# A new order of the steps of an attention group, for all engines

## The reference

```
xn = layernorm(x)
q = xn w_q (16 heads of 128), k, v = xn w_kv (4 groups of 128)
ctx = softmax(causal(q k^T / sqrt(128))) v        # 4 heads share one k, v
routed: 32 experts of 256, 6 per token by sigmoid scores in 4 of 8 groups
out = x + ctx w_dense + sum_e gate_e relu(xn W1_e^T)^2 W2_e^T
        + relu(xn Ws1^T)^2 Ws2^T
```

## The kernel before

| step | TensorE | ScalarE | VectorE |
|---|---|---|---|
| K, P, Q | project keys, values, queries of 512 tokens, 12 matmuls (L663 to L665, ps_s<-xT) | hi part | lo part (not P) |
| X | turn the values, 8 transposes (L955) | v_hi | v_lo |
| S | scores of one head and row, 3 or 6 matmuls (L974 to L976) | | |
| M | | | mask, negated row maximum, scores to probs (L1700) |
| E | | exponential and row sum (L1292) | |
| N | | | reciprocal of the sum (L1706), scaling (L1709) |
| T | turn one block of probabilities of four heads, 4 transposes (L987) | pT_hi (L1300) | pT_lo (L1319) |
| V | context of the block, 3 matmuls (bank<-pT) | | |
| F | | cT_hi | cT_lo |
| D | output projection, 12 matmuls (bank<-wa,cT) | | add to acc (L1740) |
| W | | hi of a fifth of the group's weights (araw) | lo |
| C | | | add one gathered expert output (L1729) |
| G | | | gate weights, first group only (L1507 to L1520) |

## Time and profile before

### The profile page before, as it was taken

One profiled execution on the slowest core, in us unless ns is written; L12 is line 12 of the kernel. 1 busy time (PEld: TensorE's weight loads), 2 busy tenths in 40 slices (PEclk: granted clock), 3 DMA queues, 4 the chain that ended last, 5 costly groups with the idle time before them and its releaser, 6 DMA issues.

```text
span 1565.0 us, 31168 instructions
## 1 busy us (share of the span) xinstructions
PE 1529.9 (98%) x8548; PEld 1302.8 (83%) x8549; DVE 1137.4 (73%) x2586; ACT 846.5 (54%) x1753; POOL 292.4 (19%) x540
## 2 busy tenths in 40 slices
PE   8998999999999999999999999999999999999998
PEld 7886988888899878788888878878878878888886
DVE  6796566666666668848858867976876884885886
ACT  4654666666766635535535635544554553553553
POOL 0002344443444310111001011011011011100101
PEclk8999999999999999999999999999999999999999
DMA  7792677777786712111112012522110210211101
GB/s 271 273 373 88 198 242 231 238 244 229 234 252 204 233 41 62 48 34 54 40 34 67 20 60 62 179 87 87 34 54 27 67 47 27 60 35 39 48 28 61
DMA packets 64774, 184.34 MB, mean 118 GB/s; under 512 B 7136, under 2 KB 7264, under 8 KB 60000
## 3 DMA queue, kind: packets, MB, share of 16 engines
q1 hardware_dynamic: 39888, 112.56, 20.7%
q0 software_dynamic: 16640, 54.54, 12.9%
q10 hardware_dynamic: 8208, 16.78, 2.8%
HBM read 123.29 MB, written 60.56 MB: 117 GB/s over the span
## 4 chain that ended last, share of the span: by engine, by line
PE 89%; DVE 7%; issue 2%; ACT 1%; DVEq 0%; DMA 0%; ACTq 0%; POOLq 0%; another core or an unknown queue 0%
PE bank L663 8%; PE bank L987 8%; PE bank L665 8%; PE bank L664 7%; PE ps_s L663 6%; PE ps_s L665 6%; PE ps_s L664 6%; PE ps_s L976 4%; PE ps_s L975 4%; PE ps_s L974 4%; PE ps_s L855 4%; PE ps_s L878 3%; PE ps_s L859 3%; PE ps_s L856 3%; PE ps_s L879 3%; PE ps_s L882 3%
## 5 line engine op out<-in xcount | busy, mean ns | idle before, releaser
L1292 ACT ACTIVATE probs<-probs,negmax 128x128 f32<-128x128 f32 (+7 forms) x256 | 198.2, 774 | 212.4 <-DVE negmax L1700 208.8
L1319 DVE TENSOR_TENSOR pT_lo<-bank,pT_hi 128x512 fp32r<-128x512 f32 x288 | 196.4, 686 | 99.5 <-ACT pT_hi L1300 99.1
L1300 ACT ACTIVATE pT_hi<-bank 128x512 fp32r<-128x512 f32 x288 | 167.6, 591 | 111.8 <-PE bank L987 111.1
L1700 DVE CUSTOM_DVE_ANT_0 probs<-ps_s,causal 128x128 f32<-128x128 f32 (+7 forms) x256 | 187.3, 750 | 8.3 <-PE ps_s L976 5.9
L987 PE MATMUL bank<-ident,probs 128*128 128x128 f32 x1152 | 169.7, 275 | 10.9 <-DVE pT_lo L1319 6.4
L987 PEld LDWEIGHTS bank<-ident,probs 128*128 128x128 f32 x1152 | 138.6, 141 | 49.7 <-DVE pT_lo L1319 15.6
L425 POOL TENSOR_TENSOR settled<-ident 128x1 f32<-128x1 f32 x192 | 51.5, 268 | 680.9 <-DVE acc L1729 671.2
L663 PE MATMUL ps_s<-xT_hi,wa_hi 128*128 128x512 f32 x384 | 154.3, 402 | 0.0
L665 PE MATMUL ps_s<-xT_hi,wa_lo 128*128 128x512 f32 x384 | 151.3, 394 | 0.0
L664 PE MATMUL ps_s<-xT_lo,wa_hi 128*128 128x512 f32 x384 | 150.2, 391 | 0.0
L974 PE MATMUL ps_s<-kT_hi,qT_hi 128*128 128x512 f32 (+5 forms) x384 | 138.2, 360 | 3.0 <-DVE negmax L1700 1.6
(11 more groups left out here) (197 smaller groups left out, 3602.8 us busy)
## 6 DMA issues: line engine op xcount, KB each, us to landing
eraw<-we SPq DMA_DIRECT2D x37, 1024.0 KB
expert_outputs<-ysb SPq DMA_DIRECT2D x111, 256.0 KB
araw<-wa SPq DMA_DIRECT2D x37, 512.0 KB, 4.4
expert_outputs<-comb ACTq DMA_DIRECT2D x1, 16384.0 KB, 49.0
normed_tokens<-xn SPq DMA_DIRECT2D x4, 1024.0 KB, 9.2
out<-acc SPq DMA_DIRECT2D x16, 256.0 KB
acc<-x SPq DMA_DIRECT2D x2, 1024.0 KB, 15.4
turned_tokens<-xT_hi SPq DMA_DIRECT2D x2, 1024.0 KB, 5.5
```

What stands on the lines that cost most here:

```text
L1292: act.activation(pr, pr, ACT.Exp, bias=negmax[:, i % 2, a:a + 1], scale=-1.0, accum_out=rowsum[:, i % 2, a:a + 1]).then_inc(exp_ready, 1)
L1300: act.activation(pT_hi[:, blk % RING, :], ps_t[blk % 2][:, :], ACT.Copy).then_inc(pt_hi_ready, 1)
L1319: dve.tensor_tensor(out_, whole, upper.bitcast(F32), ALU.subtract).then_inc(signal, 1)
L1700: dve.tensor_tensor_reduce(halves(probs[:, i % 2, a, 0:keys]), ps_s[:, s:s + parts, 0:keys // parts], halves(causal[:, SQ - keys:]), -1.0, ...
```

## The change

Only the two strings are changed. The same steps stand in them in another order; the waits, the operands, the instructions of each step and the transfers are as before. Since each engine takes its own steps out of the string, all three lists change.

```
 GROUP_ORDER = (
-    "S10 M10 E10 S11 M11 N10 T00 C0 E11 W3 Q10 S12 M12 W4 E12 S13 M13 N11 E13 N12 N13 Q11 S20 M20 V00 E20 S21 M21 "
-    "E21 N20 F0 Q12 T10 S22 M22 S23 M23 E22 D0 E23 C1 N21 T11 N22 S30 M30 S31 M31 E30 N23 C2 Q13 N30 V10 E31 V11 F1 "
-    "T20 S32 M32 N31 T21 E32 S33 M33 N32 T22 E33 V20 D1 N33 S40 M40 S41 M41 E40 V21 N40 T30 E41 C3 V22 F2 S42 M42 "
-    "T31 E42 S43 M43 N41 V30 N42 W0+ T32 E43 N43 D2 S50 T33 M50 V31 S51 M51 E50 T40 V32 N50 V33 F3 E51 S52 M52 T41 "
-    "T42 E52 S53 M53 E53 N51 V40 T43 N52 V41 N53 T44 S60 M60 S61 M61 V42 D3 E60 T50 N60 V43 E61 T51 V44 F4 S62 M62 "
-    "S63 M63 E62 T52 V50 E63 N61 V51 T53 S70 N62 T54 S71 V52 T55 M70 M71 N63 V53 C4 V54 W1+ D4 E70 C5 T60 V55 F5 T61 "
-    "S72 M72 N70 E71 T62 E72 C6 V60 V61 S73 M73 W2+ N71 N72 T63 E73 T64 C7 D5 K0+ V62 K1+ V63 P0+ V64 N73 T65 C8 T66 "
-    "P1+ T70 V65 V66 T71 F6 Q00+ Q01+ C9 Q02+ T72 Q03+ V70 T73 V71 T74 S00+ M00+ V72 T75 V73 V74 T76 C10 E00+ T77 "
-    "C11 V75 D6 N00+ V76 V77 S01+ M01+ F7 S02+ M02+ E01+ X+ S03+ M03+ E02+ N01+ E03+ N02+ N03+ D7"
+    "M10 M11 W3 N10 M12 E10 Q10 S10 S11 T00 S12 M13 M20 N11 C0 M21 N12 Q11 N13 S13 S20 V00 N20 N21 E11 W4 S21 E12 E13 "
+    "S22 M22 E20 M23 E21 Q12 S23 C1 F0 E22 N22 M30 M31 E23 Q13 N23 T10 T11 M32 S30 S31 E30 D0 S32 E31 T20 V10 V11 N30 "
+    "F1 M33 N31 M40 S33 N32 S40 T21 E32 T22 N33 C2 C3 E33 E40 M41 M42 V20 D1 E41 V21 S41 S42 V22 T30 T31 F2 S43 S50 "
+    "E42 M43 N40 N41 T32 E43 T33 N42 N43 V30 D2 W0+ V31 S51 M50 M51 V32 V33 T40 T41 F3 S52 N50 S53 M52 E50 E51 T42 "
+    "T43 M53 C4 V40 D3 N51 N52 M60 E52 E53 S60 T44 E60 N53 M61 V41 F4 V42 S61 V43 V44 T50 T51 S62 S63 M62 M63 E61 N60 "
+    "T52 T53 V50 E62 E63 N61 N62 N63 S70 V51 T54 T55 W1+ V52 S71 V53 V54 M70 T60 M71 T61 N70 E70 V55 D4 F5 T62 S72 C5 "
+    "W2+ M72 M73 S73 N71 N72 N73 E71 E72 E73 T63 V60 T64 V61 V62 D5 K0+ T65 V63 T66 V64 K1+ P0+ T70 P1+ V65 V66 F6 "
+    "T71 T72 Q00+ Q01+ C6 V70 T73 V71 Q02+ Q03+ T74 V72 T75 V73 V74 S00+ T76 T77 C7 C8 D6 M00+ M01+ E00+ V75 C9 M02+ "
+    "F7 E01+ E02+ N00+ N01+ V76 S01+ N02+ M03+ N03+ V77 S02+ S03+ C10 E03+ C11 X+ D7"
 )
-FIRST_ORDER = ("K0 G0 K1 G1 P0 G2 P1 G3 Q00 G4 Q01 G5 Q02 Q03 S00 M00 E00 S01 M01 E01 N00 X S02 M02 E02 N01 S03 M03 E03 N02 N03")
+FIRST_ORDER = (
+    "G0 G1 K0 K1 G2 G3 G4 P0 G5 P1 Q00 Q01 Q02 Q03 M00 M01 X N00 E00 E01 E02 N01 M02 S00 S01 S02 E03 S03 M03 N02 N03"
+)
```

## The result

The changed kernel takes 1537.32 us, the median of four runs (1535.63 to 1538.73). The kernel before took 1562.94 in the four runs beside it (1560.05 to 1565.0). The ratio is 0.9834, 95% interval 0.9819 to 0.9849: 25.6 us faster. The forecast was 1541 us and faster; the range was 1534 to 1557.

What follows compares the result with a forecast made beforehand. TensorE's in-order list with its waits was taken to bound the kernel. Loop 14.0, head 4.4 and tail 3.4 sum to 21.8 us, giving 1545.0 against the profiled 1566.8, so 1541 for the median; range 1534 to 1557.

Steps and rivals of the forecast that it cites:

- The bound: Whole kernel: costs are waits in TensorE's in-order list alone; any order can return at most 28 us, 1.8%.
- The loop: Seven groups of the loop: 2.4 us of waits each go, about 0.4 is lost anew; gain 14.0 us.
- narrow places: Places in the new group order with under 0.3 us in hand; expected to lose about 0.4 us per group.
- T60 and T62: Two transpose steps in row 7 on TensorE, held up by VectorE: waits of 0.52 and 0.88 + 0.25 us go.
- T43, T22, V30: Three TensorE steps in each group, waiting 0.26 us each on late VectorE work; all three waits go.
- The head: Ahead of the loop, from the end of projection Q03 to S12: 5.6 us lost, 1.2 left, gain 4.4 us.
- S12 over 4 us earlier: Sign at the head: projections K0 to Q03 end at the same time and S12 starts over 4 us earlier.
- The tail: Last group, with no following group to fill it: 6.0 us lost, 2.6 left, gain 3.4 us.
- The gathers: Gathers into three comb buffers, landing 3.4 to 6.5 us after issue: cost nothing; without cover, up to 1 us per group.
- A: Rival, chance .16: partial gain; narrow places cost 1 to 1.8 per group and clock falls at head; 1549 to 1557.
- B: Rival, chance .11: no change; every wait removed comes back elsewhere, 2.4 us per group; 1558 to 1567 us.
- C: Rival, chance .09: slower; VectorE over 2.3 us late makes TensorE's T65 wait in 8 groups; 1568 to 1575 us.

Runs made afterwards that it cites:

- e8: Changed kernel with VectorE's F7 ahead of M02 and M12 behind T00's copy, and TensorE's S12 behind Q11; 1542.72 us, ratio to before 0.9853.
- e9: Changed kernel with a group's end rearranged: TensorE runs S01 behind V77 and X ahead of S03, VectorE's steps reordered too; 1536.84 us, ratio to before 0.9829.
- e3: Kernel before with VectorE's N63 and the pT_lo of T60 and T61 ahead of C4, C5 and W1 in row 7; 1570.54 us, ratio 1.0045.
- e6: Kernel before with VectorE's C4 behind M53, C5, C6 and W2 behind T62, T60 and T61 ahead of W1; 1557.79 us, ratio 0.9964.
- e7: As e6, with the W1 step behind T62 as well, on VectorE and ScalarE; 1562.54 us, ratio to before 0.9991.
- e1: Kernel before with only the new order of the first group, ahead of the loop; 1562.23 us, ratio to before 0.9998.
- e4: Changed kernel with five unused reductions (5.63 us) added on VectorE before M72 in every group; 1589.29 us, ratio to before 1.0182.
- e10_spare: Changed kernel with one never-used tile of 32 bytes a partition allocated ahead of the attention tiles; 1542.27 us, ratio to before 0.9872.
- e5: Changed kernel with two unused reductions (2.26 us) added on VectorE before M72 in every group; 1542.78 us, ratio to before 0.9854.

## Why the prediction was right, step by step

**The bound.** TensorE's list with its waits sets the end; that held up to the last matmul. The bound of 28 us on what an order can return was nearly reached there, 27.05, but only because the bound was itself too low: the loop's part in it is 7 x 2.4, and with 7 x 3.1 it is 33.

**The loop** was forecast at 7 x (2.4 - 0.4) = 14.0 us and gave 2.73 + 16.44 = 19.2, 7 x 2.7. The second term, the loss in the new order's narrow places, was forecast at 0.4 and measured 0.24 + 0.13 = 0.37, but only the places were right. S12 does wait for M10. D7 waits, by e8 and e9, on the chain from V77 and not on F7's place behind M02. V74 on T74's pT_lo never waits. The first term was mis-sized: the period of 125.40 less the 122.3 of work is 3.1, not 2.4. I had counted the gaps of 0.25 and more. By starts a group of before also has six of 0.04 to 0.06, 0.32 together, and some 0.3 spread over hundredths, which I had named only as a bound; they went as well. The work of 122.3 was in the prediction, so the period less the work would have given the right term. That is the step that failed, by 0.7 us in each of seven groups. The period was forecast at 123.4 and is 122.7.

**T60 and T62** went, as walked. The trace has T60's pT_lo on VectorE at 885.88 and T62 at 888.79, 2.9 us later by start; the forecast had 68.1 and 71.2, which is 3.1. e3, e6 and e7 add what the prediction didn't say, that none of three smaller moves does it.

**T43, T22, V30** went: no start in a group of the changed kernel is over 0.06 us late but those of S12 and D7.

**The head** was forecast at 4.4 and gave 3.96. Waits left were forecast as 0.7 before S00 and 0.3 before S02, and are recorded as 0.54 and 0.22; the missing 0.4 is S12's wait (0.20, 0.45 by starts), the same narrow place as in the loop. The sign "S12 over 4 us earlier" was narrowly missed by that. In the sum 5.6 - 1.2 the 1.2 stands for the waits left, of which the text names 1.0. The clock's own 1.2 was nearly right: e6 and e7, with the head of before but a clock of 1.00, have S12 1.1 us earlier. In the changed kernel the clock stayed at its upper level, 2.4 GHz, and e1 shows the other case, with 0.57 over 8 us around a wait of 1.61. The rule of the Trainium skill ("TensorE: Matmul & The Clock Gate", HAM oscillation), that idle gaps put the array back to half clock and cost again behind the gap, fits before, e1, e3 and e4; but in e6 and e7 the same waits of 1.41 and 1.6 us before S00 and S10 were followed by no fall, so part of the head's gain depends on the execution.

**The tail** was forecast at 3.4 and gave 3.92: V70 waits 0.63 where 0.7 was said, and D7 1.41 (1.6 by starts), as said. The rest is again the small gaps. Behind the last matmul 1.5 of it is lost again, which the forecast didn't have.

**The gathers** were put at nothing, and in the loop they cost nothing. In the last group VectorE's C10 and C11 wait 0.16 and 1.01 us for theirs; C11 is done at 1531.87, before the last matmul ends, so that costs nothing either. But the forecast asked only when the gathered rows are needed, and not what GpSimd does after its last gather: the closing drain now ends the kernel, 1.5 us later than the last store would.

**The rivals.** A and B fell with the period. C's mechanism is real, and its size nearly right (2.67 us in hand, 2.3 forecast), but in the loop it is at K0 and not at T65. Its price was too low: 5.6 us late were to give 8 x 3.3, and e4 shows about twice that. Of its 6.6 us a period 3.1 are at K0, 1.6 to 1.9 before S12 behind a late M10, 1.1 to 1.4 the clock in all periods but one, and 0.4 the unused tile (last experiment).

**The sum** was 21.8 us, measured 27.05 in the profile up to the last matmul and 25.6 in the medians. The first term of the loop, mis-sized, gave 5.2 more than forecast, the tail 0.5 more and the head 0.4 less, and 1.5, the drain, was missing on the other side. So the forecast's 1541 is nearer to 1537.3 than its loop was, by the luck of an error on the other side.

## What to carry to other kernels

Where one engine's in-order list bounds a loop, take the loss of an iteration as its period less the work at the spacing of starts, not as the sum of the waits that the trace names; here that is 3.1 against 2.4 us, and the difference was the error of the forecast. Before moving a step ahead of a wait, list what is between its old place and its new one and who asks for each next: moved within the full stretch or behind it, N63, C and W1 mostly chose another T or K0 to wait, and ahead of it, together, they leave no wait there. Look also at what an engine off the path does last: a late last gather moved the end of the kernel. A short stall that reordering the late engine doesn't cure may be a chain of latencies, as the one before D7 was, and wants more of the bound engine's own work beside it.

## What was not expected of the hardware

**An unused tile** of 32 bytes a partition costs 0.4 us of a group of 122.7, in the matmuls alone (e10_spare, above). It had blurred e4 and e5, where it came with the added work: of e5's 0.5 us a group 0.4 is the tile. When kernels with different tiles are compared, that much is not the edit.

**The clock behind one and the same wait.** In e4 K0 waits 2.96 us in every group of the loop. In the third group (912.29 us, shown above) the matmuls behind it start 0.23 apart, as ever, at a clock of 1.00. In the other six the clock goes to 0.50, its lower level of 1.2 GHz, between 0.4 us ahead of the wait's end and 1.4 us behind it. In the fourth group they start 0.40 to 0.43 apart for 2.8 us:

```profile
1040.48 0.79 PE L666 MATMUL ps_s<-xT_hi,wa_hi 128*128 128x512 f32 x1 [2.96 <-DVE negmax L1706]
1041.07 0.63 PE L667 MATMUL ps_s<-xT_lo,wa_hi 128*128 128x512 f32 x1
1041.49 0.63 PE L668 MATMUL ps_s<-xT_hi,wa_lo 128*128 128x512 f32 x1
```
```profile
1040.50:1043.30 2.80, 2.80 (x7) 2.25 (x8) 2.73 (x6) 2.09 (x4) 0.00 (x0) 0.50 0.00 0
```

So such a wait may cost its own length or 1.4 us more (the seven gaps behind it are 1.5 us over 0.23 each, against 0.10 in the third group), and the wait's length alone does not tell which. The head says the same of shorter waits: 1.41 and 1.6 us before S00 and S10 come with a fall in before and e3, and with none in e6 and e7.
